# Attention weighing: values and turned scores in whole fp32 on two column halves of TensorE, in place of two fp32r parts on the whole array

## The reference, cut

```python
# block 4 (block 1: no bias on the scores, 8 heads, + bo at the end)
q = _split_heads(queries @ Wq.T, N_HEAD, D_KEY)
k = _split_heads(keys @ Wk.T, N_HEAD, D_KEY)
v = _split_heads(values @ Wv.T, N_HEAD, D_VALUE)
scores = jnp.einsum('bhqd,bhkd->bhqk', q, k) * D_MODEL ** (-0.5) + attn_bias
weights = jax.nn.softmax(scores, axis=-1)
out = jnp.einsum('bhqk,bhkd->bhqd', weights, v)
...
return out @ Wp.T
```

## Time and profile before

| | us |
|---|---|
| median of 3 runs | 2344.03 (2343.56 to 2344.45) |
| the profiled execution, its span | 2342.4 |
| PE busy | 2133.2 (91%) |
| PEld busy | 1771.3 (76%) |
| DVE busy | 1689.1 (72%) |
| ACT busy | 1246.3 (53%) |

### The profile page before, as it was taken

How to read it: one execution, slowest core, us unless ns; L and a number is a source line. 1 busy time by engine, 2 the same in 40 slices (tenths; PEclk the granted TensorE clock), 3 DMA queues, 4 the chain that set the end, 5 groups by cost and what they waited for, 6 DMA issues and landing times. The chain is left out here.

```text
span 2342.4 us, 39197 instructions
## 1 busy us (share of the span) xinstructions
PE 2133.2 (91%) x13794; PEld 1771.3 (76%) x13794; DVE 1689.1 (72%) x2979; ACT 1246.3 (53%) x2038; POOL 174.9 (7%) x162
## 2 busy tenths in 40 slices
PE   7999999999858889899999999999999999999636
PEld 4789778977738768578877897788877887788524
DVE  5877787778586446677778777877787778777672
ACT  3665656565630135366565656565656565656401
POOL 0000000000040034000000000000000000000000
PEclk9999999999978679999999999999999999999757
DMA  2000020000010062000000000020000000000001
GB/s 92 8 12 11 4 78 11 11 4 7 5 40 1 2 222 75 5 8 12 11 4 7 11 11 4 7 83 11 8 3 11 11 11 0 11 11 5 19 0 45
DMA packets 21376, 52.35 MB, mean 22 GB/s; under 512 B 3523, under 2 KB 6100, under 8 KB 20820
## 3 DMA queue, kind: packets, MB, share of 16 engines
q1 hardware_dynamic: 20864, 51.60, 6.2%
q10 hardware_dynamic: 468, 0.16, 0.0%
HBM read 51.23 MB, written 0.52 MB: 22 GB/s over the span
## 5 line engine op out<-in xcount | busy, mean ns | idle before, releaser
L505 ACT ACTIVATE biased_turned_hi<-ps 128x512 fp32r<-128x512 f32 x512 | 298.9, 598 | 276.4 <-PE ps L394 273.2
L624 DVE TENSOR_TENSOR biased_turned_lo<-ps,biased_turned_hi 128x512 fp32r<-128x512 f32 x512 | 340.9, 686 | 35.0 <-ACT biased_turned_hi L505 20.0
L613 DVE CUSTOM_DVE_ANT_0 biased_scores<-ps,bias 128x1024 f32<-128x1024 f32 x256 | 312.0, 1219 | 32.3 <-issue 21.5
L497 ACT ACTIVATE biased_scores<-biased_scores,biased_ntop 128x1024 f32<-128x1024 f32 x256 | 291.9, 1146 | 75.4 <-DVE biased_ntop L619 75.4
L407 PE MATMUL ps<-biased_turned_hi,biased_values 128*128 128x256 f32 x1024 | 307.9, 324 | 15.4 <-DVE biased_turned_lo L624 15.4
L394 PE MATMUL ps<-ident,biased_scores 128*128 128x128 f32 x2048 | 299.0, 274 | 1.6 <-ACT biased_scores L497 1.6
L380 PE MATMUL ps<-biased_keys,biased_queries 128*128 128x512 f32 x1024 | 280.0, 396 | 3.1 <-DVE biased_keys L586 2.4
L394 PEld LDWEIGHTS ps<-ident,biased_scores 128*128 128x128 f32 x2048 | 244.0, 141 | 34.4 <-issue 9.8
L407 PE MATMUL ps<-biased_turned_lo,biased_values 128*128 128x256 f32 x1024 | 265.4, 282 | 0.0
L365 PEld LDWEIGHTS ps<-weights_again,context_again 128*128 128x128 f32 x2048 | 232.3, 192 | 12.0 <-DVE biased_values L592 10.3
L365 PE MATMUL ps<-weights_again,context_again 128*128 128x128 f32 x2048 | 235.6, 276 | 4.0 <-DVE biased_values L592 4.0
(11 more groups left out here) (362 smaller groups left out, 3271.2 us busy)
## 6 DMA issues: line engine op xcount, KB each, us to landing
context<-in_ctx_t SPq DMA_DIRECT2D x8, 1024.0 KB, 9.2
moe_w<-in_moe_w SPq DMA_DIRECT2D x32, 256.0 KB, 2.7
context_again<-in_ctx_t SPq DMA_DIRECT2D x8, 1024.0 KB, 9.8
weights_again<-in_wqkv SPq DMA_DIRECT2D x16, 384.0 KB, 3.0
bias<-in_fside SPq DMA_DIRECT2D x1, 4096.0 KB, 23.2
biased_w_out<-in_w_out SPq DMA_DIRECT2D x16, 256.0 KB, 2.6
weights<-in_wqkv SPq DMA_DIRECT2D x8, 384.0 KB, 2.9
plain_w_out<-in_w_out SPq DMA_DIRECT2D x8, 256.0 KB, 2.4
```

Of the source, the lines that this page charges most:

```text
L497: act.activation(at, at, ACT.Exp, bias=ntop[:, qt:qt + 1], accum_out=part[:, head, qt, chunk:chunk + 1]).then_inc(exp_done, 1)
L505: act.activation(PH[:, t % 4, :, :].rearrange("p a n -> p (a n)"), c.ps[:, 4 + g % AHEAD, :], ACT.Copy).then_inc(turned_high, 1)
L613: ins = dve.tensor_tensor_reduce(at, slot(SCORES[head], i), BIAS[:, qt, chunk * KC:(chunk + 1) * KC], 1.0, -3.0e38, ALU.add, ALU.max, peak)
L624: dve.tensor_tensor(PL[:, t % 4, :, :].rearrange("p a n -> p (a n)"), c.ps[:, 4 + g % AHEAD, :], PH[:, t % 4, :, :].rearrange("p a n -> p ...
```

## The change

The values and the turned scores are kept as whole fp32 and not split. Weighing becomes two fp32 matmuls for a step, with 64 columns of weights each: the even key block's result goes to PSUM partitions 0 to 63 and the odd one's to 64 to 127, so each uses one half of the array's columns. Four steps (eight matmuls) are weighed in one go. To that end four steps are turned ahead (`AHEAD`), still through three banks (`BANKS`), into eight places in SBUF (`PLACES`). The copies out of PSUM are ACT's alone; DVE's `turned_lo` and `values_lo` are gone, and DVE waits for `turned` before it overwrites a chunk of `E`.

```diff
--- before.py
+++ after.py
@@ -191,7 +191,7 @@
-    AHEAD = 3
+    AHEAD, BANKS, PLACES = 4, 3, 8
...
-        VS = sb("values", [P, KT, 2, 2, HD], F32R)
+        VS = sb("values", [P, KT, 2, HD])
         E = sb("scores", [P, 2, S2])
-        PH = sb("turned_hi", [P, 4, 2, S], F32R)
-        PL = sb("turned_lo", [P, 4, 2, S], F32R)
+        PT = sb("turned_kept", [P, PLACES, 2, S])
...
-        FREE_PLACES, FREE_BANKS = 4, AHEAD
+        FREE_PLACES, FREE_BANKS = PLACES, BANKS
...
                 def turn(m, head, g):
 
-                    before = g - AHEAD if g >= AHEAD else max(n - NG for n in range(NG) if n % AHEAD == g)
-                    pe.wait_ge(turned_low, 2 * NG * m + NG * head + before + 1 + FREE_BANKS)
+                    before = g - BANKS if g >= BANKS else max(n - NG for n in range(NG) if n % BANKS == g)
+                    pe.wait_ge(turned_kept, 2 * NG * m + NG * head + before + 1 + FREE_BANKS)
...
-                            last = pe.transpose(c.ps[:, 4 + g % AHEAD, kt * S + qt * P:kt * S + (qt + 1) * P],
+                            last = pe.transpose(c.ps[:, 4 + g % BANKS, kt * S + qt * P:kt * S + (qt + 1) * P],
...
@@ -401,13 +400,11 @@
-                    pe.wait_ge(turned_low, 2 * NG * m + t + FREE_BANKS + 1)
+                    pe.wait_ge(turned_kept, 2 * NG * m + t + FREE_BANKS + 1)
                     for kt in range(2):
-                        for n, part_of in enumerate((PH, PL)):
-                            last = pe.matmul(c.ps[:, 7, head * S:(head + 1) * S],
-                                             VS[:, 2 * g + kt, head, :, :].rearrange("p a d -> p (a d)"),
-                                             part_of[:, t % 4, kt, :], start=(g == 0 and kt == 0 and n == 0),
-                                             stop=(g == NG - 1 and kt == 1 and n == 1))
+                        last = pe.matmul(c.ps[kt * HD:(kt + 1) * HD, 7, head * S:(head + 1) * S],
+                                         VS[:, 2 * g + kt, head, :], PT[:, t % PLACES, kt, :],
+                                         start=(g == 0), stop=(g == NG - 1))
                     last.then_inc(weighed, 1)
 
@@ -416,12 +413,15 @@
                 def attend(m, head, beside):
 
-                    for g in range(NG):
-                        if AHEAD <= g + 2 < NG:
-                            turn(m, head, g + 2)
-                        weigh(m, head, g)
-                        if g % 2 and beside:
-                            beside(g // 2)
+                    for q in range(NG // AHEAD):
+                        for n in range(2):
+                            for g in range(AHEAD * (q + 1) + 2 * n, AHEAD * (q + 1) + 2 * n + 2):
+                                if g < NG:
+                                    turn(m, head, g)
+                            if beside:
+                                beside(2 * q + n)
+                        for g in range(AHEAD * q, AHEAD * (q + 1)):
+                            weigh(m, head, g)
...
-                def values_hi(m, j):
+                def values_out(m, j):
                     act.wait_ge(values_done, NKC * m + j + 1)
-                    act.activation(VS[:, j * (KC // P):(j + 1) * (KC // P), :, 0, :],
-                                   slot("values", j).rearrange("p (n h d) -> p n h d", h=2, d=HD),
-                                   ACT.Copy).then_inc(values_high, 1)
+                    act.activation(VS[:, j * (KC // P):(j + 1) * (KC // P), :, :].rearrange("p n h d -> p (n h d)"),
+                                   slot("values", j), ACT.Copy).then_inc(values_kept, 1)
...
-                def turned_hi(m, head, g):
+                def turned_out(m, head, g):
                     t = NG * head + g
                     act.wait_ge(turned, 2 * NG * m + t + 1)
 
-                    act.wait_ge(weighed, 2 * NG * m + t + FREE_PLACES - 3)
-                    act.activation(PH[:, t % 4, :, :].rearrange("p a n -> p (a n)"), c.ps[:, 4 + g % AHEAD, :],
-                                   ACT.Copy).then_inc(turned_high, 1)
+                    act.wait_ge(weighed, 2 * NG * m + t + FREE_PLACES - PLACES + 1)
+                    act.activation(PT[:, t % PLACES, :, :].rearrange("p a n -> p (a n)"), c.ps[:, 4 + g % BANKS, :],
+                                   ACT.Copy).then_inc(turned_kept, 1)
...
-                def values_lo(m, j):
...
-                def turned_lo(m, head, g):
-                    t = NG * head + g
-                    dve.wait_ge(turned_high, 2 * NG * m + t + 1)
-                    dve.tensor_tensor(PL[:, t % 4, :, :].rearrange("p a n -> p (a n)"), c.ps[:, 4 + g % AHEAD, :],
-                                      PH[:, t % 4, :, :].rearrange("p a n -> p (a n)").bitcast(F32),
-                                      ALU.subtract).then_inc(turned_low, 1)
...
                 def attend(m, head, beside):
 
-                    for g in range(AHEAD, NG):
-                        turned_lo(m, head, g)
-                        if g % 2 and beside:
-                            beside(g // 2 - 1)
-                    if beside:
-                        beside(NSC - 1)
+                    for i in range(NSC):
+                        dve.wait_ge(turned, 2 * NG * m + NG * head + GC * (i // 2 + 1))
+                        beside(i)
```

More of the change, by code:

```diff
@@ L229, in cross_attention @@
         keys_high, keys_high_b, keys_kept = sem("keys_high"), sem("keys_high_b"), sem("keys_kept")
-        values_high, values_kept = sem("values_high"), sem("values_kept")
+        values_kept = sem("values_kept")
         scores_kept, top_done, exp_done = sem("scores_kept"), sem("top_done"), sem("exp_done")
         total_done, share_done = sem("total_done"), sem("share_done")
-        turned, turned_high, turned_low = sem("turned"), sem("turned_high"), sem("turned_low")
+        turned, turned_kept = sem("turned"), sem("turned_kept")
         weighed, o_kept = sem("weighed"), sem("o_kept")
@@ L519, in high_parts @@
                     for g in gs:
-                        turned_hi(m, head, g)
+                        turned_out(m, head, g)
                 def exponentials(m, head, chunks):
@@ L587, in keys_lo @@
                                       ALU.subtract).then_inc(keys_kept, 1)
-                def values_lo(m, j):
-                    kts = slice(j * (KC // P), (j + 1) * (KC // P))
-                    dve.wait_ge(values_high, NKC * m + j + 1)
-                    dve.tensor_tensor(VS[:, kts, :, 1, :],
-                                      slot("values", j).rearrange("p (n h d) -> p n h d", h=2, d=HD),
-                                      VS[:, kts, :, 0, :].bitcast(F32), ALU.subtract).then_inc(values_kept, 1)
                 def queries_lo(m):
@@ L645, in add @@
                                                  op0=ALU.mult, op1=ALU.add).then_inc(x_added, 1)
-                def low_parts(m, head, gs):
-                    for g in gs:
-                        turned_lo(m, head, g)
                 def attend(m, head, beside):
-                    for g in range(AHEAD, NG):
-                        turned_lo(m, head, g)
-                        if g % 2 and beside:
-                            beside(g // 2 - 1)
-                    if beside:
-                        beside(NSC - 1)
+                    for i in range(NSC):
+                        dve.wait_ge(turned, 2 * NG * m + NG * head + GC * (i // 2 + 1))
+                        beside(i)
                 norm_vector_moments(c, dve, k)
@@ L676, in _ @@
                 maxima(START, 0)
-                values_lo(START, 0)
-                values_lo(START, 1)
-                low_parts(START, 0, range(AHEAD))
-                values_lo(START, 2)
-                values_lo(START, 3)
                 with dve.Fori(START, END - 1) as m:
@@ L687, in _ @@
                     keys_lo(m + 1, 1)
-                    low_parts(m, 1, range(AHEAD))
                     add(m, 0)
@@ L695, in _ @@
                     sums(m, 1)
-                    values_lo(m + 1, 0)
-                    values_lo(m + 1, 1)
-                    low_parts(m + 1, 0, range(AHEAD))
                     add(m, 1)
-                    values_lo(m + 1, 2)
-                    values_lo(m + 1, 3)
                 m = END - 1
@@ L706, in _ @@
                 add(m, 0)
-                low_parts(m, 1, range(AHEAD))
-                attend(m, 1, None)
                 sums(m, 1)
```

10 lines of the change are left out of this document (5 added, 5 removed).

## The result

The changed kernel takes 2407.70 us in the median (four runs, 2407.16 to 2408.51), the kernel before 2344.24 beside it (2343.56 to 2346.68): ratio 1.027, 95% interval 1.0256 to 1.0283. It is slower by 63.5 us, where 83 were forecast. One run of the third experiment (4406.25 us) stands far from every other run and is left out of what follows.

A forecast was written before the change was run, and what follows sets the result against it. The prediction took the kernel to be bound by PE. To a span of 2342.4 us it added 36 for weighing and 47 for the joints: 2425 us, a median of 2427 us, 3.5% slower, own range 2405 to 2455.

The forecast's parts named there:

- Removed: DVE's splits: DVE's 768 subtractions and 96 of the values go; 527 us and more of busy time, costed at nothing beside PE.
- the chain: Forecast's sequence of waits and work at each joint, between attending and making keys or values; keys 2 start at 1572.64.
- Weighing, the streaming: In weighing four steps, the two column halves overlap fully: 1.73 us, against 1.88 before.
- Weighing, the change of shape: Each weighing group switches into halves (0.14 us) and back (0.20); group 2.07 against 1.88, +36 us over 192 groups.
- The fourth turning ahead: At joints between attending and making keys or values, PE waits for ACT's copy of step 0: 2.15 us an iteration, +47 us.
- strict order: Rival, in weighing: halves start strictly in program order, a group takes 1.94 us; 2468 us, chance 0.12.
- no overlap: Rival, in weighing: the two halves do not run at once, +369 + 47, 2760 us; chance 0.03.
- faster: Rival, in weighing: a 64-column fp32 record streams in half the time, 0.108 us; 2260 us, chance 0.09.
- The rival of the clock: PE's longer waits, 1.6 us after keys 1, lower the clock for 5 us an iteration: +55 us, 2482; chance 0.08.
- the changes of shape are hidden: Rival, around weighing: loads before them hide the array's switches, -29 + 47, 2362 us; chance 0.05.

The follow-up runs named there:

- third experiment: Changed kernel, but weighed in 384 groups of two steps in place of 192 groups of four: 2425.62 us, ratio 1.0349.
- tenth experiment: Changed kernel with a useless DVE subtraction behind only the first six chunks of scores of each attending, none in the openings: 2407.44 us, ratio 1.0265.
- eleventh: Kernel before the change (split parts, whole array), but with four steps turned ahead at the joints over three banks: 2448.85 us, ratio 1.0448.
- ninth: Changed kernel with a useless DVE subtraction behind each of the 384 chunks of scores: 2431.95 us, ratio 1.0369.
- first experiment: Changed kernel, but all eight matmuls of a group go to one half of the columns, the next group's to the other: 2736.18 us, ratio 1.1674.
- sixth: Changed kernel, but DVE instead of ACT makes the copies of steps 0 and 4 of each head: 2367.00 us, ratio 1.0098.
- seventh: Changed kernel with DVE copying steps 0 and 4, and each head's first group weighed before the second chunk of scores: 2338.06 us, ratio 0.9973.
- second experiment: Changed kernel, but the column half changes after each step (four records), not after each key block (two records): 2415.07 us, ratio 1.0304.
- fifth: Changed kernel, but only three steps are turned at the joints; the fourth is turned where attending begins: 2367.78 us, ratio 1.0099.
- fourth: Changed kernel with 16 places for turned scores, weighed in 96 groups of eight steps: 2407.24 us, ratio 1.0266.

## Why the prediction was right or wrong

Direction, bound and mechanism were right: PE stayed the bound, lost 3.0 us an iteration (3.7 forecast), part in weighing and part in four waits at the joints. The size was 20 us too high, and 2407.7 lies at the very edge of the prediction's own range of 2405 to 2455: 15 us of the 20 are the change of shape, some 2 the joints, and some 2 what was in neither term.

- *"Removed: DVE's splits", at nothing.* Right where it was put, while attending: the tenth experiment adds most of the work back and next to nothing moves. At the joints the chain already left `turned_lo` out; the eleventh shows that this is worth some 1.5 us an iteration. Not right for the openings, which I did not look at; the ninth shows DVE binding there. But between the first scores and the values nothing is turned or split for weighing, so the change took nothing from there either: 12.95 us, and 13.1 before.
- *"Weighing, the streaming", 1.73 us.* Right: eight pairs at 0.216. The first experiment shows the other half to be worth 1.72 us a group.
- *"Weighing, the change of shape", 0.34, and with it +0.19 a group, +36 us.* This is the term that was mis-sized. The pair of changes costs 0.32 (third experiment), but the work grew by only 0.11 a group, 192 x 0.11 = **+21 us**. A group of after is 2.03 us, not 2.07: its period of 5.63 less sixteen transposes at 0.109 and two times 0.93. And before's weighing was a little longer than the 1.88 that my subtraction left: attending head 0, which has no wait, is 20.81 us, less thirteen turnings at 0.436 and eight chunks at 0.925 leaves 7.74, or 1.94 for four steps. That is 0.09 a group, and with the first keys and values, 0.2 us longer together in an iteration, the 0.11 is met.
- *"The fourth turning ahead", 2.15 us an iteration, +47 us.* Right in the sum, 2.1 us, **+46 us**, and right at each joint within 0.15. By the table: after keys 1 +0.83 (forecast 0.9; keys 2 start 12.13 us after keys 0, where the chain gave 12.11), after keys 3 +0.39 (0.3), after values 1 +0.15 (0.1), after values 3 +0.71 (0.85). The last is too large for two small reasons: the chain had the values end at 1616.6, and ACT's copy start 2.36 us on, where it starts 1105.62 - 1103.37 = 2.25 us behind them; and wait and weight load cost 0.11 us from the copy's end, not 0.15 (see the end). The sixth and seventh experiments take the cause away, ACT's late first copy, and the waits all but go.
- *What was in neither term.* 22 x 3.0 = 66 us, and the spans differ by 63.7. The last head of a block has no scores beside it, and PE waits for the engines behind it: from its last score record to its last weighing the final iteration takes 27.1 us against 29.0 before. That gain I had not looked for; that it comes from the splits is likely and was not tried.

Of the rivals, strict order is refuted by the second experiment, no overlap and "faster" by the first. The clock was 1.00 in the loop of the changed kernel, with waits of 1.7 us. The rival of the clock was not far off, though: in the eleventh the same joint holds PE for over 3 us, and the queries and the projection behind it run at the lower clock. That the changes of shape are hidden is refuted by the third.

Most expectations that missed had one fault in common: each priced the work that an edit moved and not the order that it left behind, at the joints (third, fifth and sixth), between chunks of scores (fourth) and ahead of `maxima` (ninth). The eleventh missed by 37 us, of which 26 are the clock.

## What to carry to other kernels

Taking work from an engine that isn't the bound pays only if what it frees (a bank, a queue) is on the bound engine's path, so ask of each removed instruction who waited for its end. Count changes of TensorE's shape as instructions with a price, and gather work between them, as far as other engines can follow the order this makes. Where a look-ahead is made longer than its ring of buffers, the first copy out of the ring becomes a wait of the producer: give that copy to the engine that is free at that point, and see what then stands behind it there (sixth experiment). Watch the granted clock when a wait of TensorE grows: the wait's price can be more than its length (eleventh).

## What was not expected of the hardware

- The two column halves don't just overlap: a matmul for the free half starts past records of the matmuls ahead of it that still wait for the busy one, three of them in the second experiment, at a cost of 0.05 us in a group of eight. The line L983 had hinted at it.
- A change from the whole array to halves and back (and of the kind of operands with it) costs 0.32 us, measured by doubling them. The page "TensorEngine Tiling (Array Packing)" of the Trainium skill (Key Properties) speaks of a drain at such a switch; a loss of time at each switch fits that, though no run shows that it is the drain. It is a sixth of a group of 2.03 us, and more than the 0.2 us that the halves save in streaming.
- A turning's row starts 0.65 us after the start of the copy for which it waited, whose own row lasts 0.60 us. Its weight load starts in the same moment, and the next record follows 0.165 us later in place of 0.109. So wait and load together cost 0.11 us from the copy's end, though the row of the load is 0.14 long.
- Behind a wait of over 3 us the granted clock was 0.58 for 3.76 us, in an iteration that is otherwise busy (eleventh experiment). In the changed kernel, with waits of up to 1.7 us, it was 1.00 in the whole iteration.
